# Experts' second layer turned round: weights held still, outputs transposed by DMA, quarter-array scatter

## The reference, cut to what matters

```python
gates, idx = jax.lax.top_k(affinity, CAP)            # CAP = 32, per batch and expert
expert_in = jnp.take_along_axis(x[:, None, :, :], idx[..., None], axis=2)
h = jax.nn.gelu(jnp.einsum('becd,edf->becf', expert_in, w1) + b1[None, :, None, :])   # DFF = 512
expert_out = jnp.einsum('becf,efd->becd', h, w2) + b2[None, :, None, :]
out = jnp.zeros_like(x)
out = out.at[jnp.arange(b)[:, None, None], idx].add(gates[..., None] * expert_out)
```

## Time and profile before

| | us |
|---|---|
| median of 3 runs (lowest, highest) | 1920.71 (1919.81, 1920.91) |
| span of the profiled execution | 1918.0 |
| median less span: what lies around the span | 2.7 |
| first take of the experts stage | 475.47 |
| last residual of the stage ends | 1296.5 |

### The profile page before, as it was taken

One profiled execution on the slowest core, in us unless ns is written; L12 is line 12 of the kernel. 1 busy time (PEld: TensorE's weight loads), 2 busy tenths in 40 slices (PEclk: granted clock), 3 DMA queues, 4 the chain that ended last, 5 costly groups with the idle time before them and its releaser, 6 DMA issues. The chain is left out here.

```text
span 1918.0 us, 72744 instructions
## 1 busy us (share of the span) xinstructions
PE 1812.8 (95%) x28635; PEld 1311.9 (68%) x28635; DVE 1609.1 (84%) x3645; ACT 1564.4 (82%) x2773; POOL 662.4 (35%) x918
## 2 busy tenths in 40 slices
PE   6999998896999999999999999998999999999898
PEld 4777776542666666666666666766777777777677
DVE  5999987598788888888888888778999999988744
ACT  5899997575998989898989989876888888888543
POOL 4788887231000000000000000004666666655565
PEclk8999999897999999999999999999999999999899
DMA  7644545495000000000000001004665555533233
GB/s 180 130 99 93 103 94 102 139 364 187 14 11 15 13 14 11 15 13 15 10 14 14 13 12 52 2 2 107 153 169 154 144 156 147 154 69 72 64 111 121
DMA packets 312954, 160.67 MB, mean 84 GB/s; under 512 B 236558, under 2 KB 295862, under 8 KB 312374
## 3 DMA queue, kind: packets, MB, share of 16 engines
q1 hardware_dynamic: 312278, 157.95, 31.4%
q10 hardware_dynamic: 480, 0.05, 0.0%
HBM read 62.33 MB, written 36.83 MB: 52 GB/s over the span
## 5 line engine op out<-in xcount | busy, mean ns | idle before, releaser
L1793 DVE TENSOR_TENSOR h<-g,h 128x1024 f16<-128x1024 f32 x256 | 313.3, 1224 | 138.3 <-ACT h L1725 138.0
L239 PEld LDWEIGHTS psE<-ew,h 128*128 128x128 f16 x6144 | 351.2, 98 | 56.0 <-issue 40.1
L239 PE MATMUL psE<-ew,h 128*128 128x128 f16 x6144 | 365.2, 219 | 12.8 <-DVE eo L1803 6.0
L1720 ACT ACTIVATE g<-psH,eb1T 128x512 f32<-128x512 f32 x512 | 330.2, 680 | 30.9 <-PE psH L239 24.5
L814 POOL TENSOR_TENSOR Ph<-E,Ph 128x512 f16<-128x512 f32 x192 | 222.0, 1156 | 235.9 <-ACT Ph L768 235.9
L1866 POOL MEMSET rbias<- 64x384 f32 x1 | 0.4, 411 | 839.2 <-POOLq L133 839.2
L1725 ACT ACTIVATE h<-g 128x1024 f16<-128x1024 f32 x256 | 270.6, 1057 | 8.1
L720 ACT ACTIVATE vB<-psV 128x512 f16<-128x512 f32 x384 | 225.9, 589 | 51.2 <-PE psV L618 49.0
L841 DVE TENSOR_TENSOR vB<-psV,vB 128x512 f16<-128x512 f32 x384 | 248.4, 678 | 1.1 <-ACT vB L720 1.0
L618 PE MATMUL psV<-shared 96*64 96x512 f16 x1536 | 209.9, 379 | 1.5 <-DVE vB L841 1.5
L820 POOL TENSOR_TENSOR E<-E,rden 128x512 f32<-128x512 f32 x192 | 199.7, 1040 | 15.1 <-DVE rden L852 14.3
(11 more groups left out here) (308 smaller groups left out, 3417.9 us busy)
## 6 DMA issues: line engine op xcount, KB each, us to landing
keys_ahead<-shared SPq DMA_DIRECT2D x52, 512.0 KB, 4.8
shared<-keys_ahead SPq DMA_DIRECT2D x52, 512.0 KB, 3.6
rawe<-in_L_ffn_w_dram SPq DMA_DIRECT2D x32, 256.0 KB, 3.1
wb<-rw SPq DMA_DIRECT2D x64, 128.0 KB, 2.0
rows<-places SPq DMA_DIRECT2D x110, 64.0 KB, 2.5
out_dram<-x SPq DMA_DIRECT2D x7, 512.0 KB, 3.2
context_T<-shared SPq DMA_DIRECT2D x64, 48.0 KB, 2.4
PT<-Ph SPq DMA_TRANSPOSE x192, 2.8
```

Source lines behind the costliest of these rows:

```text
L239: last = e.matmul(to, a, b, start=start and n == 0, stop=stop and n == 2, **flags)
L1720: e.activation(g32[:, ft, :], psH[:, ft, :], ACT.Gelu_apprx_tanh, bias=b1T[:, a.expert(1) * FT + ft:a.expert(1) * FT + ft + 1]).then_inc(s ...
L1793: e.tensor_tensor(h[:, 1 - par, 1, 2 * q:2 * q + 2, :], g32[:, 2 * q:2 * q + 2, :], h[:, 1 - par, 0, 2 * q:2 * q + 2, :], ALU.subtract)\
```

## The change

1. The second layer holds w2 still and lets h move: 12 products of 512 columns in place of 48 of 128. Its output `psE` is now transposed: 128 features by 512 rows.
2. The gating multiplies by a row of gates that is the same on all 128 partitions, `grow`. For this SP stores the gate values in DRAM once (`gate_rows`, 16 transfers) and loads 256 KB in every step, each row repeated on all partitions, in turn into two buffers.
3. The hi and lo halves of the gated outputs move to GpSimd (a copy and a subtraction of 128x512). They are written side by side, 32 hi columns and 32 lo columns of each batch, in one buffer, `eoT`.
4. One DMA transpose in each step turns `eoT` (128x1024 f16) into `eoZ`, in which 64 partitions hold the hi and lo rows of one batch.
5. The scatter becomes 16 products with 64 contracted rows and 64 output rows; it runs two bodies after its step in place of one, and stands between the first and the second layer instead of behind the second. An extra body is added at the end.
6. `put` is made by one comparison of 128x512 in place of four of 128x128. `residual` moves from body e=1 to e=2, the statistics from odd to even e. SP's loop over tiles becomes a loop over bodies.

```diff
             def body(a):   # TensorE
...
-                            for ft in range(FT):
-                                last = matmul3(e, psE[:, r, :],
-                                               [h[:, par, hl, ft, r * P:r * P + P] for hl in range(2)],
-                                               [w2[:, hl, a.expert(0), ft, :] for hl in range(2)],
-                                               r == ft == 0, ft == FT - 1, skip_group_check=True)
-                        if a.has(-1):
-                            wait(e, s["put"], j - 1, RT)
-                            wait(e, s["eo_lo"], j - 1)
+                        if a.has(-2):
+                            wait(e, s["put"], j - 2)
+                            wait(e, s["turned"], j - 2, 16)
...
                             for r in range(RT):
-                                for hl in range(2):
+                                for turn in range(2):
                                     for bp in range(2):
+                                        side = (bp + turn) % 2
                                         rows = slice(64 * bp, 64 * bp + 64)
-                                        last = e.matmul(psA[:, bp, r, :], put[rows, r, :], eo[rows, hl, r, :],
+                                        to = slice(64 * side, 64 * side + 64)
+                                        last = e.matmul(psA[to, bp, r, :], put[rows, RT * side + r, :],
+                                                        eoZ[rows, RT * side + r, :], start=False,
...
+                        if a.has(0):
+                            wait(e, s["h_lo"], j, 2)
+                            wait(e, s["gated"], j - 1)
+                            for ft in range(FT):
+                                last = matmul3(e, psE[:],
+                                               [w2[:, hl, a.expert(0), ft, :] for hl in range(2)],
+                                               [h[:, par, hl, ft, :] for hl in range(2)],
+                                               ft == 0, ft == FT - 1)
...
                     def body(a):   # SP
+                        if a.has(-1):
+                            wait(e, s["eo_lo"], j - 1)
+                            wait(e, seeded["A"], j - 2)
+                            e.dma_start_transpose(eoZ[:], eoT[:].rearrange("p b l c -> p (b l c)"))\
+                             .then_inc(s["turned"], 16)
+                        if a.has(1):
+                            load_gates_of(j + 1)
...
+                @block.gpsimd
+                def _(e):
+                    for n in range(NE * NG):
+                        wait(e, s["gated"], j)
+                        wait(e, s["turned"], j - 1, 16)
+                        e.tensor_copy(eoT[:, :, 0, :], exact).then_inc(s["eo_hi"], 1)
+                        wait(e, s["eo_hi"], j)
+                        e.tensor_tensor(eoT[:, :, 1, :], exact, eoT[:, :, 0, :], ALU.subtract)\
+                         .then_inc(s["eo_lo"], 1)
...
                 # ScalarE
-                                e.activation(eo[:, 0], eo32[:], ACT.Copy).then_inc(s["eo_hi"], 1)
...
                 # VectorE
-                            for r in range(RT):
-                                e.tensor_scalar(put[:, r, :], iota[:],
-                                                tok_slot[:, a.expert(-1), a.group(-1) * RT + r:a.group(-1) * RT + r + 1],
-                                                None, ALU.is_equal).then_inc(s["put"], 1)
+                            e.tensor_tensor(put[:], iota[:, 0:N].unsqueeze(1).broadcast_to([P, GT, N]),
+                                            of_step.unsqueeze(2).broadcast_to([P, GT, N]), ALU.is_equal)
...
-                            e.tensor_tensor(eo[:, 1], eo32[:], eo[:, 0], ALU.subtract)\
-                             .then_inc(s["eo_lo"], 1)
```

## The result

The kernel after the change takes 1939.45 us (median of 4 runs, 1935.56 to 1943.09), the kernel before in the same session 1920.26 us (1917.07 to 1920.91). The ratio is 1.0099, with a 95% interval of 1.0081 to 1.0117: slower by 1%. The forecast was 1930, slower; the sign and the range held, the size is half of what came: +9 against +19 by the medians and +21.4 by the two profiled spans, 1918.0 and 1939.4.

A forecast was written before the change was run, and what follows sets the result against it. TensorE's products set the pace, with a wait for VectorE's queue in each second step. Steady -5, heads +6, port +2, tail +3.5, loads +2.5 sum to +9: 1918.0 + 9 + 2.7, about 1930 us, range 1905 to 1975.

The forecast's parts named there:

- Second layer and scatter: TensorE's products: layers 2.69 us each, scatter 0.37, both with 0.09 for a shape change; TensorE alone 6.06 a step.
- Rival B: Scatter on TensorE: quarter products no faster than half ones, +11 us, 1941; chance 0.17.
- put and its wait: VectorE's put takes 0.60 us behind the gating; the scatter waits 0.58 for it, making a pair of steps 12.70.
- rival C: put on VectorE at half the price, 0.35 us: 16 us less, 1914; chance 0.16.
- The steady term of -5: Pairs of steps in the experts stage: 12.70 against 12.77 us, 4 to 7 us won over 112 steps, 5 taken.
- The shared port: GpSimd's operations and VectorE's two-SBUF-input ones shut each other out, mostly covered: 2 us, between 0 and 7.
- The heads: Seven group heads: residual now stands ahead of put in body 2; net 0.9 us each, 6 us (3 to 12).
- The loads: Last group: loads for the next stage stand ahead of one transpose, plus 2.5 us.
- The tail: End of the stage: last step goes through gating, GpSimd, transpose and scatter, 6.3 us for 2.9: plus 3.5.
- The transpose: DMA transpose of eoT lands in 3.1 us; from gating to landing 5.2, fitting with 0.7 us to spare.
- Rival A: Single eoT and eoZ: transpose loop becomes the bound from a landing of about 3.5 us; 1975 at 4.0; chance 0.13.
- Rival D: put is never late, so a step is TensorE's 6.06 us: 36 us less, plus 6 for ends, 1891; chance 0.12.

The follow-up runs named there:

- e8: The changed kernel with put computed for four of its eight token blocks only, the rest zero: 1922.13 us.
- e10: The changed kernel with the scatter's 16 products made half-array ones (64 rows to 128 outputs): 1952.01 us.
- e3: The changed kernel with GpSimd's copy and subtraction done on one sixteenth of the operand only: 1923.63 us.
- e5: The changed kernel with the scatter back behind the second layer and the four loads spread over bodies 1, 3, 5 and 7 of the last group: 1908.23 us.
- e6: e5 with two eoT tiles in turn, so GpSimd's copy waits for the transpose of two steps ago: 1889.16 us.
- e7: e6 with VectorE's selection of the next tile's tokens moved ahead of put: 1886.81 us.
- e4: The changed kernel with the four next-stage loads issued one each in bodies 1, 3, 5 and 7 of the last group: 1932.31 us.
- e9: The changed kernel with two eoT tiles in turn, scatter still ahead of the second layer, loads still together: 1943.49 us.

## Why the prediction was half right

- *Second layer and scatter: right.* From start to start the full-array layers are 2.60 behind one another and 2.69 ahead of the scatter, 0.09 for a change of shape, as forecast; the scatter is 0.35 (forecast 0.37). TensorE alone needs 6.06 us a step, to the digit of the forecast, and sets the short step of each pair by it (e8, e10). Rival B, that quarter products are no faster, is refuted by e10.
- *put and its wait: right.* put by itself is 0.68 us, as long as the f32 gating; rival C is out as a fact, and e8 gives the worth of half of put as 18.8 us, forecast 16. Ordinary pairs are 12.60 to 12.67, forecast 12.70; the wait in the long step is 0.47 to 0.55, forecast 0.58.
- *The steady term of -5: wrong, by what it was held against.* The 12.70 of an ordinary pair was compared with 12.77, which is the mean of the kernel before with its heads in it. An ordinary pair of that kernel is 6.15 + 6.44 = 12.59, and the 0.42 that the prediction calls the mean wait of a pair is 0.29 there; the rest are the heads. So the prediction's own 12.70 says that each pair loses 0.11, some 6 us in all, where the sum has 5 won. It lost 0.01 to 0.08.
- *The shared port: the step that failed most.* "I take 2 us in all, between 0 (the cover holds everywhere) and 7." e3 measures 16.4, at least 12.6 of them ahead of the last group. The mechanism was seen and its cover misjudged: I asked whether ScalarE was waited for anyway behind h_low, and did not follow put, which stands last in the queue that TensorE waits for, nor the selection, which I took for exempt. Some 8 us of it lie at the six heads ahead of the last group's, where residual, put and GpSimd's two operations stand together, and of these 3.4 are the clock lost at two of them.
- *The heads: right by luck.* The forecast has +0.9 for each. They came out as 0.0 to +0.6 with the clock kept and +1.9 and +2.3 with the clock lost (26.67 before), +1.0 in the mean. Without GpSimd's work it is -0.4, so the whole of it is what the port and the clock cost, and the forecast had only priced residual and put.
- *The loads: right mechanism, half the size.* 2.5 forecast, 6.0 measured. I counted the delay of the transpose, not that TensorE comes back from such an idle time at the lower clock (5.04 us for 2.76).
- *The tail: 3.5 forecast, 4.4 measured*; GpSimd's blocked subtraction is in it (1.68 for 1.16).
- *The transpose: right.* Landing in 3.1 us, fitting as long as the scatter stands first. Rival A was priced at a landing of 3.5; e5 and e6 show that its loop depends as much on where the scatter stands.
- *Rival D, the waits vanish*, did not come, but e7 shows it was the better kernel: 1886.8, where D called 1891. What it took was not in the change: order on TensorE, the loads, one more tile.

Of the 10 to 12 us by which the forecast fell short, 5 are the steady part and heads with the port in them (8.2 for the 3 of the sum), 3.5 the loads, 1 the tail; the rest, up to 3, lies in untouched stages and in the difference of spans and medians. That the 5 are so few is in part luck. With GpSimd's work small the stage takes 2.6 us more than before the change (822.2 against 819.6), where the sum without its port term has 7: the rest of the sum was 4.4 too high and the port term 14 too low.

## What to carry to other kernels

When work goes to GpSimd, list what VectorE has in that time, its fast one-input comparisons too, and follow each to whoever waits for it: the same 1.85 us of GpSimd a step cost 16 us in one arrangement of the program and nothing in another. Compare like with like: an ordinary pair with an ordinary pair, not with a mean that has the heads in it. A product that needs a late operand belongs behind one that doesn't, here 26 us for moving 16 products past 12. And after a change of order ask which single buffer now closes a loop: the second eoT won nothing with the scatter first and 19.1 us with it last.

## What the runs showed of the hardware

- VectorE and GpSimd shut each other out from both sides: subtraction 1.16 us alone, up to 2.02 beside h_low; h_low 1.23 alone, 2.17 beside it; a one-input f16 comparison 0.34 alone, 1.24.
- From start to start 16 f16 products with 64 contracted rows and 128 columns take 0.35 us with 64 output rows (the changed kernel) and 0.56 with 128 (e10), each with a full-array layer behind them.
- After idling for 1.72 us TensorE ran its next layer partly at the lower clock in two heads (4.45 us for 2.76, granted clock 0.61) and at full clock in three. In e4 and e9 it is two of five and two of six. Heads with waits of 0.9 to 1.5 us kept the clock in every trace. What decides it stays open.
- A transpose issued behind 2 MB of loads landed after 9.1 us, beside a load of 256 KB after 3.1 (median).
